# A self-attention block with talking heads: learnt keys first in tiles of 128+128+16, queries by row halves, 17 steps a batch, and other stages' work inside the step loop

## The reference, cut to what matters

```python
q, k, v = heads(x @ Wq), heads(x @ Wk), heads(x @ Wv)      # 16 heads of 64
k = concat([mem_k, k], axis=2)                            # 16 learnt keys ahead of 256 tokens
v = concat([mem_v, v], axis=2)
dots = einsum('bhid,bhjd->bhij', q, k) * 64 ** -0.5
dots = einsum('bhij,hk->bkij', dots, pre_proj)            # mix the heads before the softmax
attn = softmax(causal(dots), axis=-1)
attn = einsum('bhij,hk->bkij', attn, post_proj)           # and after it
out = einsum('bhij,bhjd->bhid', attn, v)
return merge(out) @ Wo
```

## Time and profile before

| | us |
|---|---|
| median of three runs (lowest, highest) | 1503.5 (1502.05, 1507.72) |
| the profiled execution's own time | 1501.14 |
| its span, first to last instruction | 1499.4 |
| cross attention, up to | 1126.9 |
| self attention | 1127 to 1402.8 |
| feed-forward, from | 1403.1 |

### The profile page before, as it was taken

The page is one execution under the profiler, slowest core; times in us unless marked ns, Lnnn a source line. Parts: engine busy times, 40 slices in busy tenths (PEclk is TensorE's granted clock), DMA queues, the critical chain, the costliest instruction groups (busy, mean ns, idle before and its releaser), DMA issues. The chain is left out here.

```text
span 1499.4 us, 21539 instructions
## 1 busy us (share of the span) xinstructions
PE 1344.5 (90%) x8543; PEld 987.8 (66%) x8543; DVE 908.8 (61%) x1155; ACT 736.3 (49%) x1313; POOL 396.0 (26%) x342
## 2 busy tenths in 40 slices
PE   3999999999999998999999999999986978899643
PEld 3787776868777675868686776868672546564322
DVE  5556667675666766476667567576755545170476
ACT  3555656555565655555555655555542333140152
POOL 3505234250523423232415143241503000000000
PEclk9999999999999999999999999999996979985676
DMA  4202031120302132202112020211205341500000
GB/s 143 71 2 74 1 75 33 43 62 14 74 1 71 30 102 60 71 2 74 47 29 75 1 74 1 75 46 26 60 1 158 39 53 24 62 8 1 21 0 15
DMA packets 41958, 68.12 MB, mean 45 GB/s; under 512 B 4737, under 2 KB 30849, under 8 KB 41601
## 3 DMA queue, kind: packets, MB, share of 16 engines
q1 hardware_dynamic: 41856, 66.73, 18.8%
HBM read 25.82 MB, written 0.52 MB: 18 GB/s over the span
## 5 line engine op out<-in xcount | busy, mean ns | idle before, releaser
L447 DVE TENSOR_REDUCE step_max<-score_banks 128x2 f32<-128x1024 f32 x256 | 299.1, 1220 | 126.0 <-PE score_banks L571 126.0
L468 DVE TENSOR_TENSOR prob_sum<-prob_sum,probs 128x1024 f32<-128x1024 f32 x224 | 279.2, 1288 | 139.7 <-ACT probs L398 139.0
L398 ACT ACTIVATE probs<-score_banks 128x1024 f32<-128x1024 f32 x181 | 181.8, 1028 | 149.2 <-PE out_ps L597 85.3
L330 POOL TENSOR_TENSOR k_split<-probs,k_split 64x512 fp32r<-64x512 f32 x128 | 163.5, 1278 | 330.5 <-ACT probs L381 325.5
L585 PE MATMUL score_banks<-q_twice,k_split 128*128 128x256 f32 x724 | 182.2, 288 | 0.2 <-ACT probs L398 0.2
L586 PE MATMUL score_banks<-q_low_max,k_ones 128*128 128x256 f32 x724 | 178.1, 283 | 0.0
L332 POOL TENSOR_TENSOR k_split<-probs,k_split 64x512 fp32r<-64x512 f32 x128 | 164.0, 1281 | 9.6
L585 PEld LDWEIGHTS score_banks<-q_twice,k_split 128*128 128x128 f32 x724 | 138.4, 191 | 11.9 <-issue 6.2
L586 PEld LDWEIGHTS score_banks<-q_low_max,k_ones 128*128 128x128 f32 x724 | 138.5, 191 | 0.0
L373 ACT ACTIVATE k_split<-key_banks 64x512 fp32r<-64x512 f32 x128 | 75.6, 591 | 120.7 <-PE key_banks L534 120.2
L323 POOL TENSOR_TENSOR w_lo<-w_raw,w_hi 128x768 fp32r<-128x768 f32 x16 | 36.1, 2257 | 354.6 <-ACT w_hi L349 354.6
(11 more groups left out here) (199 smaller groups left out, 2374.5 us busy)
## 6 DMA issues: line engine op xcount, KB each, us to landing
k_ones<-k_split SPq DMA_DIRECT2D x128, 256.0 KB, 3.9
ctx_rows<-in_ctx_dram SPq DMA_DIRECT2D x10, 512.0 KB, 3.9
grouped<-dots_sb SPq DMA_DIRECT2D x32, 136.0 KB
w_raw<-in_L_xattn_w_v_dram SPq DMA_DIRECT2D x14, 256.0 KB, 3.5
probs<-in_ctx_dram SPq DMA_DIRECT2D x6, 512.0 KB, 5.9
grouped<-dots_sb SPq DMA_DIRECT2D x32, 72.0 KB
w_raw<-in_L_xattn_w_q_dram SPq DMA_DIRECT2D x16, 128.0 KB, 3.6
w_raw<-in_L_xattn_w_k_dram SPq DMA_DIRECT2D x16, 128.0 KB, 3.6
```

The costliest lines, as they stand in the source:

```text
L330: pool.tensor_tensor(k_split[DH:P, A, keys], keys_staged[j % 2][0:DH], k_split[0:DH, A, keys].bitcast(F32), ALU.subtract).then_inc(k_low[A ...
L398: act.activation(probs[:, j % 2, h, :], scores_of, ACT.Exp, scale=SCALE).then_inc(exp_done, 1)
L447: dve.tensor_reduce(step_max[:, qt, :, j], score_banks[:, 2 * qt:2 * qt + 2, :], X, ALU.max).then_inc(max_done, 1)
L468: dve.tensor_tensor(prob_sum[:, h, :], prob_sum[:, h, :], probs[:, j % 2, h, :], ALU.add).then_inc(sum_done, 1)
```

## The change

What it does, stage by stage:

- The learnt keys stand first in one row of 272 keys, cut into tiles of 128, 128 and 16 (was 16, 128 and 128). `xnT` gets 16 zero columns ahead of the tokens, V is projected from it in the same tiles, and `mem_v` is written into the first 16 rows of `v_sb` by a DMA; the last 16 tokens have V tiles of their own (two more projections, one more copying DMA). So a `post` needs one product a group while `keys` <= 128 (steps 0 to 6), two up to 256, three only for the last two groups.
- No `q_padded`: each head's 64 rows of Q are multiplied with its 64 rows of K. Dots of a pair take both query tiles at once. In batch 0 they stand between the projections, and each pair's DMAs follow its copies; odd pairs go out from SP, even pairs from ACT.
- The loop has 34 steps for both batches (17 each, the last two of one group). `mix` is one product for both groups; `post` runs three iterations behind; the maximum is negated by its own instruction; the scaled Kronecker matrices are made by POOL; copies of `mixed` go to ACT for even steps and to DVE for odd ones. `mixed` is cleared by two POOL memsets that wait for the last projection.
- Inside the loop: hidden transposes (iterations 1 to 6), dots of batch 1 (8 to 15), their near DMAs (ACT's at 16) and far DMAs (ACT's at 18), products of batch 0 (20), output of batch 0 in eight parts (22 to 29). Products alternate the two heads of a pair.
- The ten loads of small constants are issued by ACT, the rest by SP.

What POOL gains and loses:

```diff
-            pool.memset(q_padded[DH:P, 0:HEADS:2, :], 0.0).then_inc(zeroed, 1)
-            pool.wait_ge(zeroed, 1)
-            pool.memset(q_padded[0:DH, 1:HEADS:2, :], 0.0).then_inc(zeroed, 1)
...
+            pool.wait_ge(proj_made, NPROJ)
+            pool.memset(mixed_first, 0.0).then_inc(mixed_zero, 1)
+            pool.memset(mixed_second, 0.0).then_inc(mixed_zero, 1)
...
+            for n in range(STEP_ALL):
+                count = len(groups_of(n))
+                pool.wait_ge(inv_done, n + 1)
+                if n >= RING:
+                    pool.wait_ge(post_made, n - RING + 1)
+                pool.tensor_tensor(kron_scaled[:, n % RING, 0:count, :],
```

What SP issues behind the weight loads:

```diff
+            for pair in range(1, PAIRS, 2):
+                sp.wait_ge(dots_copied[1], pair // 2 + 1)
+                for t in range(QT):
+                    send_dots(sp, 0, pair, t)
+
+            for eng in range(2):
+                sp.wait_ge(proj_copied[eng], NPROJ // 2)
             for b in range(BATCH):
...
+                sp.dma_start(v_sb[0:MEM, b, 0, :].rearrange("p (h d) -> p h d", h=HEADS),
+                             mem_v.rearrange("h m d -> m h d")).then_inc(memv_in, 16)
+            sp.dma_start(v_last_b1[:, :], v_last[MEM:2 * MEM, :]).then_inc(last_in, 16)
+
+            for t in range(QT):
+                sp.wait_ge(mix_made, SA_STEPS // 2 if t == 0 else SA_STEPS)
+                for pair in range(1, PAIRS, 2):
+                    sp.wait_ge(dots_copied[1], PAIRS // 2 + pair // 2 + 1)
+                    send_dots(sp, 1, pair, t)
```

ACT's loop:

```diff
+            act.wait_ge(mixed_zero, 2)
+            for n in range(STEP_ALL + LAG):
+                if n < STEP_ALL:
                     exponentials(n)
...
+                if n >= LAG + 1 and (n - LAG - 1) % 2 == 0:
+                    copy_mixed(act, copy, n - LAG - 1, mixed_by_act)
...
+                u = n - DOTS_AT
+                if 0 <= u < PAIRS and u % 2 == 0:
+                    copy_dots(act, scaled_copy, PAIRS + u)
+                if n == DOTS_AT + PAIRS or n == SA_STEPS + 1:
+                    t = 0 if n == DOTS_AT + PAIRS else 1
+                    act.wait_ge(mix_made, SA_STEPS // 2 if t == 0 else SA_STEPS)
+                    act.wait_ge(dots_copied[0], PAIRS)
+                    for pair in range(0, PAIRS, 2):
+                        send_dots(act, 1, pair, t)
+                if n == FIRST_PRODUCT:
+                    for m in range(PAIRS):
+                        act.wait_ge(out_made, m + 1)
+                        copy(outT[:, m, :], bank[m % 2][:, 0:SEQ]).then_inc(out_copied, 1)
```

PE:

```diff
+            def mix(n):
...
+                if s in (0, SA_STEPS // 2):
+                    pe.wait_ge(regrouped[t], ALL_REGROUPED * (b + 1))
+                if n >= MIX_RING:
+                    pe.wait_ge(exp_done, n - MIX_RING + 1)
...
+            def post(n):
+                keys, count = keys_of(n), len(groups_of(n))
+                pe.wait_ge(kron_done, n + 1)
+                if n >= 2:
+                    for copied, steps in zip((mixed_by_act, mixed_by_dve), copies_until(n - 1)):
+                        wait_past(pe, copied, steps)
+                for tile in range((keys + P - 1) // P):
...
+            def product_with_v(b, pair):
...
+                for m, (at, v, mixed) in enumerate(parts):
+                    for half in range(2):
+                        k = 2 * pair + half
+                        last = mm(bank[n % 2][half * DH:(half + 1) * DH, at:SEQ], v[:, k * DH:(k + 1) * DH], mixed[:, k, :],
...
+            for pair in range(PAIRS):
+                project(2 * pair)
+                project(2 * pair + 1)
...
+                if pair > 0:
+                    dots(pair - 1)
+            project(NQK)
+            dots(PAIRS - 1)
+            for n in range(NQK + 1, NPROJ):
                 project(n)
...
+            pe.wait_ge(memv_in, 32)
+            pe.wait_ge(last_in, 16)
+
+            for n in range(STEP_ALL + LAG):
+                if n < STEP_ALL:
+                    mix(n)
+                if n == FIRST_PRODUCT:
+                    all_products(0)
+                if n >= LAG:
+                    post(n - LAG)
+                if HIDDEN_AT <= n < HIDDEN_AT + 2 * WT_BANKS:
+                    transpose_hidden(n - HIDDEN_AT)
+                if DOTS_AT <= n < DOTS_AT + PAIRS:
+                    dots(PAIRS + n - DOTS_AT)
+                if OUT_AT <= n < OUT_AT + 2 * 4:
+                    output(0, n - OUT_AT)
+            all_products(1)
+            for part in range(2 * 4):
+                output(1, part)
```

More of the change, by code:

```diff
@@ L1177, in project @@
-                last.then_inc(proj_made, 1)
-            def dots(n):
-                t, b, pair = n // PAIRS % QT, n // PAIRS // QT, n % PAIRS
-                keys = dot_keys(t)
-                if n >= 2:
-                    pe.wait_ge(dots_copied[n % 2], (n - 2) // 2 + 1)
-                for half in range(2):
-                    tokens = (b * QT + t) * P
-                    last = mm(bank[n % 2][:, half, 0:keys], q_padded[:, 2 * pair + half, tokens:tokens + P],
-                              kT[:, pair, b, 0:keys], start=True, stop=True)
+                    out = projection_bank(n)
@@ new lines, in project, with dots @@
+                    last = mm(out, w, a, start=(c == 0), stop=(c == DC - 1))
+                last.then_inc(proj_made, 1)
+            def dots(u):
+                b, pair = u // PAIRS, u % PAIRS
+                if u < PAIRS:
+                    for eng in range(2):
+                        pe.wait_ge(proj_copied[eng], pair + 1)
+                if u == PAIRS:
+                    pe.wait_ge(hidden_copied, 2 * WT_BANKS)
+                back = 2 if u < PAIRS else 1
+                if u >= back:
+                    pe.wait_ge(dots_copied[(u - back) % 2], (u - back) // 2 + 1)
+                for t in range(QT):
+                    at, keys = (0, NEAR)[t], dots_keys(t)
+                    tokens = slice((b * QT + t) * P, (b * QT + t + 1) * P)
+                    for half in range(2):
+                        rows = slice(half * DH, (half + 1) * DH)
+                        last = mm(dots_bank(u)[:, half, at:at + keys], qT[rows, pair, tokens], kT[rows, pair, b, 0:keys],
+                                  start=True, stop=True)
@@ new lines, in post @@
+                for tile in range((keys + P - 1) // P):
+                    rows = min(keys - tile * P, P)
+                    at = (0, 2 * P, 3 * P)[tile]
+                    for g in range(count):
+                        last = mm(post_bank(n)[0:rows, at + g * P:at + (g + 1) * P],
+                                  expd[:, n % RING, g, tile * P:tile * P + rows], kron_scaled[:, n % RING, g, :],
+                                  start=True, stop=True)
+                last.then_inc(post_made, 1)
```

592 lines of the change are left out of this document (289 added, 303 removed).

## The result

The changed kernel takes 1433.7 us (four runs, 1430.8 to 1435.3) against 1502.8 (four runs) before: ratio 0.953, 95% interval 0.951 to 0.956. That is 69 us less. The forecast was 38 less, 1465 us, and its range ended at 1440. The direction was right and the size too small. The profiled execution after took 1433.27 us, its span 1431.1, so it is compared with the 1501.1 and 1499.4 from before.

The account below looks back on a forecast made before the run. PE's work, its clock and two waits were taken to set the time. Stage estimates ended the self attention block at 1365 against 1402.8: -38 us, 1463 for the profiled execution, 1465 for the median; range 1440 to 1495.

Parts of the forecast that it names:

- Start: Block start: without POOL's clearing of `q_padded`, the first projection comes at 1136 instead of 1142, 6 us earlier.
- 1153 + 54 = 1207: First regrouping: DMAs leave at 1153 and one batch, 3.4 MB at 63 GB/s, takes 54 us, ending at 1207.
- The first rival: Regrouping: two queues are faster than one, up to 108 GB/s; middle wait 10 us, total 1449; chance 0.2.
- The wait for SP's late loads: Ahead of the first step: PE waits for `mem_v`, issued by SP behind its regrouping DMAs: 3 us more.
- the lower bound (half of 1.9): Dots of a pair: 1.9 us is the upper bound, half of it the lower if halves overlap; 1.2 taken.
- the near iterations: Batch 0 loop: eight near iterations, partly at half clock, with hidden transposes, take 16 us.
- the far ones: Batch 0 loop: nine far iterations at 2.3 us, with dots of batch 1 at 8 x 1.2, take 28 us.
- a chain through ACT and DVE: Far steps: `post` needs the copy two steps earlier, behind ACT's exponentials; 5.2 us for two steps, 2.6 each.
- Middle: Ahead of the 18th `mix`: PE waits for near DMAs of batch 1, between 9 and 27 us, 19 taken.
- the second rival: ACT and SP get in each other's way: middle wait 27 us, ACT issues at 1.18 us, total 1482; chance 0.1.
- 14 us had been taken for batch 1: End of block: products of batch 1, alternating column halves, take 14 us, between 11 at full clock and 18 at half.
- the third rival: Whole new loop: PE's clock stays at 1.2 GHz, total 1520 us, slower than before; chance 0.05.

Follow-up runs that it names:

- one queue: The changed kernel with all regrouping DMAs issued by SP, pair after pair, none by ACT: 1423.4 us, ratio 0.956.
- by head: The changed kernel with all three products of a head done before those of the next head: 1448.5 us, ratio 0.972.
- the spread kernel: The changed kernel with SP issuing all regrouping DMAs and each head's 8 rows written to partitions 16 apart: 1401.6 us; run again, 1405.9 us.
- the kernel with dots sooner: The spread kernel with three waits moved to first use, and hidden transposes and dots of batch 1 one iteration sooner: 1404.1 us, ratio 0.936.

## Why the prediction was too small

By its own steps, forecast against the profiled execution:

| stretch, us | forecast | measured | off |
|---|---|---|---|
| up to the first projection | 1136 | 1134.7 | -1 |
| from there to the first `mix` | 75 | 62.6 | -12 |
| first to last `mix` of batch 0 | 44 | 36.3 | -8 |
| from there to the 18th `mix` | 19 | 26.9 | +8 |
| iterations 17 to 24 | 37 | 34.6 | -2 |
| iterations 25 to 33 | 26 | 19.2 | -7 |
| end of the block | 28 | 22.4 | -6 |
| feed-forward | 96.3 | 94.4 | -2 |

The direction was right, but the size was not: the forecast took its unknowns to err either way, by some 20 us together, and seven of eight stretches came out short, by 30 in all even with the +8.

*Start.* Right: the subtractions went from 8.4 to 2.3 us, and the first projection moved by 7.

*First regrouping: the step that failed.* "1153 + 54 = 1207" took 63 GB/s for the rate of the DMAs, whoever issues them. The rows had one issuer, so they could not show that. The first rival saw the right sign: it named 108 GB/s as the end, 103 was reached, and one queue put back the 61 and 9 of the 12 us. Its other half, a middle wait of 10, did not come: there the queues moved 78 GB/s on average and 25.3 us passed. It had a chance of 0.2 because the share was the same for both sizes of piece; but the share of busy engines does not say why they are busy: it was the same at 61, 105 and 181 GB/s, and what changed the rate of one queue was the partitions written to. The other 3 us are an earlier start: the first regrouping DMA left at 1148.6, not 1153. The wait for SP's late loads was forecast at 3 us; 4.9 was measured, with a load behind the last copy.

*Loop of batch 0 and far steps.* Dots of a pair took 0.9 us, about the lower bound (half of 1.9); 1.2 had been taken. The drain on a change of mode that the Trainium skill states (TensorEngine Tiling (Array Packing), Key Properties) does not show in these 0.9 us. Of the -8 in batch 0, the near iterations have -1 (14.8 against 16) and the far ones -7 (21.4 against 28), dots 8 x 0.3 of it. The far steps of batch 1 were priced at 2.6 us, all nine, by a chain through ACT and DVE; there `mix` (up to 1.12 us) and posts (1.18) follow one another almost without a wait. Two full steps without an output part took 4.5 us together against the chain's 5.2, which was summed from single durations (two copies of 0.38 behind one another take 0.62). The first two and the last step, with fewer posts or one group, took only 1.0 to 1.3 beside their output parts. So the nine, with five output parts, took 19.2 us and not 26: the term was mis-sized by 0.7 us a step.

*Middle.* The wait was forecast between 9 and 27, at 19; 26.9 came from `mix` to `mix`, 25.3 of it waiting, near the end at which all must pass. The place and the cause are right: with the near DMAs sent earlier it fell to 4.45. This +8 hid a part of the other errors. It is also the first half of the second rival; its second half, 1.18 us an issue on ACT, did not come here (0.62 to 0.88).

*Products.* 14 us had been taken for batch 1, between 11 and 18; it took 8.4. All 12 records of a pair had been priced at 0.115 us; eight are so (0.90), but four have 16 columns only and take 0.07. Alternating gives half (by head 16.5), as the step said. That the clock would be up at the end, against the third rival, was right; for batch 0 it was at 0.50 behind the hole, as forecast.

*Not priced.* The prediction priced POOL's memsets beside DVE at the start, and then counted the new ones at 1192 only by their own end. They ended at 1198.8, but beside them the quantisation held DVE until 1201.3. With the quantisation moved away the loop of the changed kernel was 3.6 us shorter, though its total did not show it; in the spread kernel the same delay stood hidden behind the first wait.

## What to carry to other kernels

A DMA rate read from one queue is the rate of that pattern of addresses: before using it as a limit, ask which partitions the transfers in flight write to. Spreading a transfer's rows gave a higher rate here (181 GB/s with rows 4 apart) than a second issuer (103), and a second issuer can pay in its own stream. When a wait at the head of a loop is removed, look at every engine's stream up to its first instruction in the loop: another wait of nearly the same length may stand behind it, as DVE's quantisation did here. Price a clearing by POOL twice, by its own time and by what DVE has to do beside it.

## What the runs showed of the hardware that was not expected

The rate of one queue writing 8 rows followed from their places: 61, 105 and 181 GB/s for rows 1, 16 and 4 apart, at an engines' share of 0.54 to 0.59. A second queue raised the first to 103 where both moved data at once, and the second only to 107.

POOL's memsets and DVE's operations of L748 and L750 exclude each other rather than slow each other: L748 began at 1193.06, POOL's first memset ended at 1195.99, and L748 ended 0.81 us later, at 1196.80, about the 0.95 that it takes alone; L750 likewise ended 0.81 us behind the second memset. The second memset took 2.83 us, and 2.02 where the quantisation was moved away. They need not alternate: in the kernel with dots sooner L748 took 5.70 us, through both memsets, and again ended 0.81 us behind the second. Not all of DVE's work is held: where the quantisation was moved away, its masks took 0.20 us beside the memsets, as elsewhere. The Trainium skill, SBUF — State Buffer, section SBUF: two separate sides, says that the pair of ports that DVE and GpSimd share is locked for a whole instruction, against the DVE operations that use it; the trace agrees.
